# Local-attention layers on one core: the masks of the scores written into PSUM by ScalarE, the deviations widened by ScalarE, clamp and first guess as three-operand instructions

## The reference, cut to what matters

```python
for i in range(DEPTH):                       # DEPTH = 6
    x = attn_layer(shift_tokens(x), Wqkv[i], q_scale[i], k_scale[i], Wo[i]) + x
    x = ffn_layer(shift_tokens(x), ln_g[i], ln_b[i], W1[i], b1[i], W2[i], b2[i]) + x

# in attn_layer: 16 heads of 64, windows of 32 queries that see 64 keys
q = l2norm(q) * qs                           # q / max(|q|, 1e-12), the same for k
sim = jnp.einsum('bhwie,bhwje->bhwij', bq, bk2) * QK_SCALE
sim = jnp.where(mask, -jnp.finfo(sim.dtype).max, sim)
attn = jax.nn.softmax(sim, -1)

# in ffn_layer
var = ((x - mu) ** 2).mean(-1, keepdims=True)
xn = (x - mu) / jnp.sqrt(var + 1e-05) * g + bln
```

## Time and profile before

| | |
|---|---|
| median of 3 runs | 3918.51 us (3902.11 to 3930.37) |
| the profiled execution | 3909.73 us, span 3908.0 us |
| mean granted clock of TensorE | 0.973 |
| busy in the span: PE, PEld | 3681.3 us (94%), 2759.5 us (71%) |
| busy in the span: DVE, ACT, POOL | 3122.8 us (80%), 2478.4 us (63%), 2312.1 us (59%) |

### The profile page before, as it was taken

The page is one execution under the profiler, slowest core; times in us unless marked ns, Lnnn a source line. Parts: engine busy times, 40 slices in busy tenths (PEclk is TensorE's granted clock), DMA queues, the critical chain, the costliest instruction groups (busy, mean ns, idle before and its releaser), DMA issues. The chain is left out here.

```text
span 3908.0 us, 148870 instructions
## 1 busy us (share of the span) xinstructions
PE 3681.3 (94%) x64802; PEld 2759.5 (71%) x64802; DVE 3122.8 (80%) x5087; ACT 2478.4 (63%) x4014; POOL 2312.1 (59%) x1367
## 2 busy tenths in 40 slices
PE   6888888679999999999999999999999999999996
PEld 4555555367777777777777777777777777777774
DVE  4454444299998899999989999988899998889893
ACT  3555555357676666676666667666667676666664
POOL 1000010177777777777777777776777777777772
PEclk9999998799999999999999999999999999999998
DMA  1000000112222222222222222221222222222112
GB/s 55 4 4 4 4 4 4 41 45 55 53 61 55 59 61 56 55 56 66 58 56 53 55 53 67 58 55 48 55 64 64 55 53 53 56 60 56 51 51 69
DMA packets 123005, 188.89 MB, mean 48 GB/s; under 512 B 25054, under 2 KB 44278, under 8 KB 122108
## 3 DMA queue, kind: packets, MB, share of 16 engines
q1 hardware_dynamic: 122364, 179.36, 17.0%
HBM read 24.08 MB, written 4.19 MB: 7 GB/s over the span
## 5 line engine op out<-in xcount | busy, mean ns | idle before, releaser
L1294 POOL TENSOR_TENSOR rc<-rc,rnorm 128x1024 f32<-128x1024 f32 x384 | 731.8, 1906 | 392.1 <-DVE rnorm L172 375.0
L1288 POOL TENSOR_TENSOR rc<-rc,rs 128x1024 f32<-128x1024 f32 x384 | 911.0, 2372 | 7.2 <-DVE rs L1353 3.6
L1329 POOL TENSOR_TENSOR prob_b<-prob_b,rinv 128x1024 f32<-128x1024 f32 x192 | 365.5, 1904 | 354.9 <-DVE rinv L1434 354.9
L1347 DVE TENSOR_TENSOR rc<-proj,rope_b 128x1024 f32<-128x1024 f32 x384 | 465.5, 1212 | 85.3 <-ACT squares L1151 84.3
L724 DVE TENSOR_REDUCE negmax<-tm 128x1 f32<-128x384 f32 (+3 forms) x512 | 247.5, 489 | 344.9 <-PE tm L416 335.8
L1151 ACT ACTIVATE squares<-proj 128x1024 f32<-128x1024 f32 x384 | 392.6, 1022 | 175.3 <-PE proj L903 171.7
L994 PEld LDWEIGHTS ring<-pT,vmoved 64*64 64x64 f32 x18432 | 379.6, 135 | 135.0 <-issue 135.0
L1353 DVE TENSOR_TENSOR rs<-proj,rope_b 128x1024 f32<-128x1024 f32 x384 | 465.9, 1213 | 0.0
L1361 DVE TENSOR_REDUCE sums<-squares 128x16 f32<-128x1024 f32 x384 | 463.8, 1208 | 0.0
L940 PEld LDWEIGHTS ring<-ident,rc 128*128 128x128 f32 x3072 | 359.5, 141 | 141.4 <-issue 43.6
L940 PE MATMUL ring<-ident,rc 128*128 128x128 f32 x3072 | 425.9, 276 | 15.6 <-POOL rc L1294 12.2
(11 more groups left out here) (171 smaller groups left out, 8472.0 us busy)
## 6 DMA issues: line engine op xcount, KB each, us to landing
vmoved<-vown SPq DMA_DIRECT2D x576, 128.0 KB
vmoved<-vown SPq DMA_DIRECT2D x192, 192.0 KB
vmoved<-vown SPq DMA_DIRECT2D x576, 64.0 KB
wqkv_raw<-in_L_ffn_Wqkv SPq DMA_DIRECT2D x40, 192.0 KB, 3.0
wo<-in_L_ffn_Wo SPq DMA_DIRECT2D x6, 512.0 KB, 5.1
x_attended<-xtok SPq DMA_DIRECT2D x8, 256.0 KB, 2.0
xtok_c<-x_attended SPq DMA_DIRECT2D x8, 256.0 KB, 4.2
out<-xtok_c SPq DMA_DIRECT2D x8, 256.0 KB, 3.3
```

The source lines that it names most:

```text
L1288: nc.gpsimd.tensor_tensor(rc[:, k % 2, c, :], rc[:, k % 2, c, :], rs[:, c, :], ALU.add).then_inc(add_done, 1)
L1294: nc.gpsimd.tensor_tensor(dst, dst, rnorm[:, k % 2, c * HEADS:(c + 1) * HEADS].rearrange("p (h o) -> p h o", o=1).broadcast_to([P, HEADS, ...
L1329: nc.gpsimd.tensor_tensor(pr, pr, rinv[:, :, :].rearrange("p q (s o) -> p q s o", o=1).broadcast_to([P, PAIRS, 2, KEYS]), ALU.mult).then_i ...
L1347: nc.vector.tensor_tensor(rc[:, k % 2, c, :].rearrange("p (h d) -> p h d", h=HEADS), proj[c][:, :].rearrange("p (h d) -> p h d", h=HEADS), ...
```

## The change

The two mask matmuls of each tile go, but for the first tile. ACT writes the mask of tile `g+1` over the whole of `scr` right behind the exp of tile `g`, ahead of the copies of O0 and O1, and PE's scores wait for it. ACT takes over the widening of the deviations, ahead of the exp. The clamp and the first guess, tensor_scalar instructions before, become scalar_tensor_tensor instructions; the guess reads its constant from a tile `magic` that POOL fills once.

```diff
-            def mask_scores(k):
-                need(pe, sub_done, k)
+            def mask_first_scores():
                 for s in range(2):
-                    mask = win_mask[k % TILES].rearrange("p (o k) -> p o k", o=1).broadcast_to([P, PAIRS, KEYS])
+                    mask = win_mask[0].rearrange("p (o k) -> p o k", o=1).broadcast_to([P, PAIRS, KEYS])
                     nc.tensor.matmul(scr[:, s, :, :], ident_bf, mask, start=True, stop=True)
             def score(k, half):
                 j = k % TILES
                 pe.wait_ge(ring_free, RING[f"T{2 * half + 1}", k] + 1)
+                if half == 0:
+                    need(pe, scr_masked, k)
...
-                if tile(g):
-                    mask_scores(g)
+                if g == 0:
+                    mask_first_scores()
...
+            def widen_deviation(k):
+                act.wait_ge(rn_done, (min(k, NT) + 1) * RSQRT_STEPS)
+                nc.scalar.activation(dev, rnorm[:, k % 2, 2 * HEADS:].rearrange("p (t o) -> p t o", o=1)
+                                     .broadcast_to([P, TILES, P]), ACT.Copy).then_inc(spread_done, 1)
...
+                if seq_at(g, 6) is not None:
+                    widen_deviation(g + 1)
                 if tile(g):
                     act.wait_ge(sub_done, g + 1)
                     pr = prob[g % 2][:, :, :, :]
                     nc.scalar.activation(pr, pr, ACT.Exp).then_inc(exp_done, 1)
+                if tile(g) and tile(g + 1):
+                    mask = win_mask[(g + 1) % TILES].rearrange("p (s q k) -> p s q k", s=1, q=1)
+                    nc.scalar.activation(scr[:, :, :, :], mask.broadcast_to([P, 2, PAIRS, KEYS]), ACT.Copy).then_inc(scr_masked, 1)
                 if tile(g - 1):
                     attention_out(g - 1, 0)
                     attention_out(g - 1, 1)
...
-                    nc.vector.tensor_scalar(ss, ss, 1e-24, None, ALU.max).then_inc(clamp_done, 1)
+                    nc.vector.scalar_tensor_tensor(ss, ss, 1e-24, ss, ALU.max, ALU.max).then_inc(clamp_done, 1)
...
-                rsqrt(nc, dve, sums[:, lo:hi], rnorm[:, k % 2, lo:hi], rtmp[:, lo:hi], rn_done, i * RSQRT_STEPS)
-
-            def widen_deviation(k):
-                nc.vector.tensor_copy(dev, rnorm[:, k % 2, 2 * HEADS:].rearrange("p (t o) -> p t o", o=1)
-                                      .broadcast_to([P, TILES, P])).then_inc(spread_done, 1)
+                x, y, t = sums[:, lo:hi], rnorm[:, k % 2, lo:hi], rtmp[:, lo:hi]
+                nc.vector.scalar_tensor_tensor(y.bitcast(i32), x.bitcast(i32), -0.5, magic[:, lo:hi], ALU.mult, ALU.add).then_inc(rn_done, 1)
+                cubic(nc, dve, x, y, t, rn_done, i * RSQRT_STEPS)
+                newton(nc, dve, x, y, t, rn_done, i * RSQRT_STEPS)
+                dve.wait_ge(rn_done, (i + 1) * RSQRT_STEPS)
...
-                if seq_at(g, 6) is not None:
-                    widen_deviation(g + 1)
```

More of the change, by code:

```diff
@@ L135 @@
 RSQRT_STEPS = 1 + 4 + 3
[L138 to L144, removed]
 def first_guess(nc, x, y, sem):
@@ L728, in part_b @@
 def part_b(nc, t_in, alloc, need, resT, ident, win_mask, ident_bf, vecs):
-    f32, f32r, bf16 = mybir.dt.float32, mybir.dt.float32r, mybir.dt.bfloat16
+    f32, f32r, bf16, i32 = mybir.dt.float32, mybir.dt.float32r, mybir.dt.bfloat16, mybir.dt.int32
     ALU, ACT, AX = mybir.AluOpType, mybir.ActivationFunctionType, mybir.AxisListType
@@ L751, in part_b @@
         rtmp = sb("rtmp", [P, 2 * HEADS + TILES])
+        magic = sb("magic", [P, 2 * HEADS + TILES])
         rc = sb("rc", [P, 2, 2, INNER])
@@ L786, in part_b @@
         ring_full = sem("ring_full"); ring_free = sem("ring_free")
-        scr_full = sem("scr_full"); max_done = sem("max_done"); sub_done = sem("sub_done")
+        scr_masked = sem("scr_masked"); scr_full = sem("scr_full"); max_done = sem("max_done"); sub_done = sem("sub_done")
         exp_done = sem("exp_done"); sum_done = sem("sum_done"); inv_done = sem("inv_done"); prob_done = sem("prob_done")
@@ L1251, in _ @@
             nc.gpsimd.memset(vown[:, 1, :, :, :], 0.0).then_inc(zeroed, 1)
+            nc.gpsimd.memset(magic[:, :], float(0x5F3759DF)).then_inc(zeroed, 1)
             pool.wait_ge(consts_in, 16)
@@ L1334, in _ @@
         def _(dve):
-            dve.wait_ge(zeroed, 6)
+            dve.wait_ge(zeroed, 7)
             dve.wait_ge(consts_in, 16)
```

## The result

Before, the median was 3918.51 us; the changed kernel has 3944.72 us (3931.73 to 3950.73 in 11 runs). The ratio is 1.0066, 95% interval 1.0048 to 1.0084: slower by 26 us, less than the 1% set as the bound of "no change", and clear of the spread of the runs. The profiled execution took 3950.73 us with a span of 3949.0 us, 41 us over the one before. That pair overstates the change: the one before was 9 us under its median, the one after 6 us over its own.

A forecast was written before the change was run, and what follows sets the result against it. PE was taken to issue without pause, setting the time. The four kinds summed to +1.09 us a cycle, +0.9 with the pauses, times 48: +43 us, put at 3957 us, range 3878 to 4005.

The forecast's parts named there:

- rival (b): Mask write on ACT is short, 0.5 us, or the weighing's pauses disappear: about 0.1 us a cycle, 3914 us; chance 0.22.
- rival (c): Mask write on ACT is long, 1.3 us, or DVE and POOL fall behind: 2.1 us a cycle, 4010 us; chance 0.13.
- What bounds the kernel: Part B: PE issues without pause and what it issues sets the time; DVE is second, at 92% of a 300 us stretch.
- The mask write: ACT's write into PSUM ahead of the copies of O0 and O1: 0.96 us, bounds 0.5 and 1.3 us.
- Kind 0: One of a cycle's four kinds of step: ACT has no gap, so the mask write moves T2 by all of it, +0.96 us.
- Kind 1: One of four kinds of step: T0 0.10 us late, the mask matmuls' 0.43 us come off in full, -0.33 us.
- Part 3: The widening leaves DVE: 0.42 us a step off DVE, claimed to be worth nothing to the span.
- Kind 2: One of four kinds of step: ACT's idle time takes in the write, T2 may start earlier but T3 can't, 0.
- Kind 3: One of four kinds of step, widening also ahead of the exp: output 0.68 us late, less 0.22, +0.46 us.
- the pauses: PE's pauses within the weighing, 20 in 36 cycles: ACT is then early at O0, -0.19 us a cycle in kind 3.
- Widening and clamp: DVE work moved or reformed: widening off DVE gains nothing, clamp stays near 0.56 us; 0.37 us a step saved if it didn't wait.
- Rival (a): PE keeps all its gain, ACT's write vanishing in ACT's idle 32%: 3909.7 - 82 = 3828 us; chance 0.15.

## Why the prediction was right, and where its terms were off

The direction and the mechanism held: 26 us slower where 38 were forecast against the median (3957 to 3918.51), with the sum at +43.

The chances were less apt: slower by over 1% had 0.45, and the 0.7% measured falls under the 0.35 of "within 1%". Two slips stand in the working: in rival (b) O0 would be 0.52 - 0.14 + 0.5 = 0.88 later, not 0.86, and rival (c) comes out at 4010 us by its own sum, above a range that claims to leave out only its top.

- **What bounds the kernel.** PE issued nearly without pause, and its gaps after the change are ended by ACT's copies. But "what it issues sets the time" isn't so: part of what it issued filled time in which the ring wasn't free, and leaving out 82 us of its issue brought 36.
- **The mask write.** Taken at 0.96 us in pitch, with bounds of 0.5 and 1.3. In the rows above it is 2145.65 - 2144.70 = 0.95. The nearest row, an instruction with as many elements, was the right guide, and the write into PSUM is about as long as squares, which read from it. The sentence of the Trainium skill ("ScalarE: Activation LUTs", section "Step-by-step: what each stage is for") that a PSUM destination is the faster one has little to go by here: 1.016 us against 1.052 for the exp, which computes something else and reads fp32 instead of bf16. No run has the same copy with both destinations.
- **Kind 0**, +0.96: measured 2.89 + 1.80 - 2.50 - 1.31 = +0.88. The gap of 1.4 us that was to show ahead of T2 came in two parts, since T0 had to wait for the copy of O0 first: T0 0.39 us late, which the forecast had not, and T2 0.87 behind the end of T1 (1.31 from start to start, less 0.44 for a fill). That the net loss hangs on this term is shown by the kernel with kind 0 back on PE.
- **Kind 1**, -0.33: this is the mis-sized term. T0 came 0.22 late instead of 0.10, and the masks gave back 0.39. But the step also won 0.20 us ahead of the weighing. There PE had waited for DVE's gate in the kernel before; the row is

```profile
PEld proj L901 <- DVE hid L1400: 12.2, 28, 0.5
```

and it stood in the same view as the two PEld rows, right above them. I had passed over it, and Part 3 says that DVE ends no wait of PE. It is 12.2 us before, 12.4 without any mask, 0.2 in the changed kernel, 13.6 with kind 0 back on PE, 7.0 with the clamp that doesn't wait. When kind 0 delays PE, DVE's gate is ready in time. So about 0.2 of the 0.88 us were time that PE would have waited anyway. The changed kernel's shorter clamp is part of the same shift: for a tile of kind 1, whose clamp comes at the end of PE's step of kind 0, it starts after POOL's instruction has ended, and takes 0.19 instead of 0.63 us. By the steps of these two executions kind 1 went from 15.51 to 15.15, -0.36, so close to the forecast only because two errors met; the median step went from 15.22 to 14.62.
- **Kind 2**, 0: measured 0 (15.73 and 15.70), with the gain at T2 given back at T3.
- **Kind 3**, +0.46, less 0.19 for the pauses: T0 0.56 late in the mean. In the steps without a pause in the weighing it is 0.68 late, as forecast for the output; in the 8 of 34 with one it is 0.14 late, so the pauses took back 0.13. The masks gave 0.42 back, and P0 came 0.16 later behind the scores (forecast 0.21): 17.17 to 17.49, +0.32 in the mean of all steps. With masks and widening together this term is there, with either alone it is small.
- **Sum.** The four kinds give +0.84 + (-0.36) + (-0.03) + 0.32 = +0.77 us a cycle between tiles 44 and 179 of the two profiled executions, where +0.9 was forecast. Over the whole of part B it is 31 us (3065.9 - 3034.9), since ahead of tile 44 the kernel before had more pauses in the weighing. Of the 41 us between these two executions 8 lie ahead of part B, where the change touches nothing. The medians of all runs say 26 us. Without the pauses part B is 39 us longer, so that the total is as low as it is also by luck: the pauses took 8 us less than before, in 20 steps instead of 28, and why isn't known.
- **Widening and clamp**: what they take off DVE was priced at nothing, and measured so. The price of the widening on ACT is part of kind 3: alone it cost nothing that the runs can tell, beside the masks 13 us of part B (38.4 - 25.3) more than the two alone. That the clamp wouldn't get shorter through its form was read from short instructions with two SBUF inputs under POOL's, one of them in the earlier trace rows, and is shown now by equal 564 ns. The saving of 0.37 us a step that the prediction named for a clamp without a wait was too high: the clamp alone saves 0.35 in the mean, but what comes next takes over part of the wait. Here the rule of the Trainium skill ("SBUF — State Buffer", section "Who interferes with whom") agrees with the runs: two SBUF inputs wait, the tensor_reduce with one doesn't.
- **Rival (a)**, the faster one, would have needed the write to vanish; the kernel without any mask shows that not even then 82 us come off.

## What to carry to other kernels

Work that is taken off the busiest engine is worth only what isn't a hole: before moving it, look at what its place in the queue was hiding, here the time in which the other engine empties a buffer. Then look at what stands behind the new place on the engine that takes it; the mask write on ACT lost 8 to 12 us ahead of the copies that release the ring, and 26 us together with the widening, but was free, with a gain of 30 us, when half of the masks went into slots where ACT waits for PE and the other half stayed on PE. Two additions that are each free may share one slack, so price them together.

## What the runs showed of the hardware that was not expected

- A DVE instruction that isn't held by POOL can hand the wait on to one behind it. For tiles of kind 2 clamp, guess and the instruction of line 156 took 0.77, 0.92 and 0.19 us before (medians of 34), and 0.21, 0.53 and 0.93 with a clamp that doesn't wait: of 0.56 us saved on the clamp 0.21 are left over the three.
- PE pauses for up to 1.7 us in the middle of the weighing, with nothing in the trace that releases it, in every kernel (15 to 28 times in 2300 us), whether PE waited elsewhere or not. Over part B they took 24 us in the trace of one kernel (masks alone) and 42 in that of another (kind 0 back on PE), though the two kernels are only 9 us apart, so they bear on comparisons of this size. What they are was not tried and stays open.
